# Keys and queries of two 16-head cross stages, held by head in row groups of TensorE

## The chip, the cores and the metric

The kernel runs on one core of a Trainium2 chip, as one program with one launch. The metric is the device time of one execution in microseconds; the median of three runs of the kernel before is 626.02 us (623.32 to 626.36).

## What is computed

The reference is a small transformer of twelve stages over `x` (128 rows of 128 numbers) with a context of 2048 rows of 128. Each stage adds its output to `x`. The stages are called here l0x, l0a, l0f, l1x, l1a, l1f, l2x and so on: cross attention, self attention and a feed-forward part, four times. The change is in l1x and l2x, two cross attentions of 16 heads with 8 numbers each:

```python
q = (Q @ Wq.T + bq).reshape(m, -1, H, HD)          # 128 queries, H = 16, HD = 8
k = (K @ Wk.T + bk).reshape(m, -1, H, HD)          # 2048 keys
v = (V @ Wv.T + bv).reshape(m, -1, H, HD)
energy = jnp.einsum('mqhd,mkhd->mhqk', q, k) * SCALE
energy = jnp.where(mask == 0, jnp.float32(-1e+20), energy)
attn = jax.nn.softmax(energy, axis=3)
out = jnp.einsum('mhqk,mkhd->mqhd', attn, v)
```

l2x is the same without biases and without a mask.

## The kernel before

Five engines run instruction lists written out by hand, one function per stage (`l0x`, `l0a`, ...) with a part for each engine (`@on("pe")` and so on). Engines wait for each other through semaphores that are planned by name (`Steps`). Both cross stages are one function, `cross` (L1159; its part for TensorE begins at L1192).

The products of queries and keys are made to nearly full precision from parts in the type fp32r: a number is split into a high and a low part. For a quad (four heads, `QUADS` = 4) the contraction has 105 rows (`SHOWN`): 32 rows high keys, 32 rows high keys again, 32 rows low keys (4 heads of 8 each), and 9 rows for the mask and for a shift by the maximum. Against them stands `query_r`, in which each of the 16 heads has its own 128 columns and zeros in the rows of the other three heads of its quad; `spread` (L1187) writes it, one quad on VectorE (DVE), three on GpSimd (POOL).

A stage goes twice over the scores. The first pass (`peak`) needs only the maximum of each query and head: for head h and half a, two matmuls of 512 keys each (L1218) fill two PSUM banks, and one VectorE reduce over 1024 columns (L1312) takes the maximum. There are 32 such steps in a stage. When the eight of a quad are done, `lows` is formed, `shift_gpsimd` splits it, `turn` puts it on rows by a matmul and `place` (L1325) writes it into `query_r`, so that the second pass yields scores minus the maximum.

The second pass (`score`, `weigh`) goes over 64 units, a quad and 128 keys each: one matmul, keys as weights (128 columns) and 512 columns of queries (4 heads); ScalarE (ACT) takes the exponential (L1371) from one of three PSUM banks into `probs`; `weigh` multiplies with the values in fp32, four matmuls for two units, each into its own 32 output columns of the array. `take` gathers a quad, `fold` brings the heads together.

The order on TensorE (PE) is written out: peaks 0 to 8, the first shift, two scores, peak 10, then 32 rounds v of two scores, peak v + 11 (while there are any: 21 rounds), and `weigh` of two units. Matmul records all carry line L257 (`mm`), transposes L260.

The keys come by 12 DMAs of 256 KB for each stage from `stack_keys` on SyncE's queue (SP), which copies rows from the tiles with high and low parts; l2x has one more for the constant rows.

## Time and profile before

| | |
|---|---|
| median of 3 runs | 626.02 us |
| the profiled execution | 628.98 us |
| its span, first to last instruction | 626.9 us |
| mean granted TensorE clock | 0.892 of 2.4 GHz |
| PE busy | 501.0 us (80%) |
| DVE busy | 355.9 us (57%) |
| ACT busy | 230.4 us (37%) |
| l1x / l2x, from the end of the stage before to their last sum | 80.6 to 161.9 us / 243.7 to 322.4 us |

The profile gives busy time by engine, the chain of waits that ended last, groups of instructions with their mean duration, a timeline, and busy time and granted clock for any stretch. Matmuls overlap in their pipeline, so the record of one is longer than the distance to the next; distances between starts are what counts.

### The profile page before, as it was taken

The numbers are of one execution on the slowest core, as the hardware profiler recorded it, in microseconds if no ns is written. First come the engines' busy times: TensorE is split into PE (matmuls) and PEld (weight loads), VectorE is DVE, ScalarE is ACT, GpSimd is POOL, SyncE is SP. The second block draws the span as 40 slices with busy tenths as digits, with TensorE's granted clock in tenths as the row PEclk, the third lists the DMA queues.
The fourth block names the chain that finished last, engine by engine and source line by source line (L and its number), as shares of the span: only waits on it lengthen the run. The fifth ranks groups of instructions, "written<-read, shape, count | busy, mean of one in ns | idle before, by whom it ended". The sixth has DMA issues, their size and how long they took to land.

```text
span 626.9 us, 9025 instructions
## 1 busy us (share of the span) xinstructions
PE 501.0 (80%) x3612; PEld 375.2 (60%) x3612; DVE 355.9 (57%) x795; ACT 230.4 (37%) x443; POOL 57.4 (9%) x103
## 2 busy tenths in 40 slices
PE   7778659999758707899987667778999999887786
PEld 5646534444538606444345457766888888776686
DVE  5465458771569325877446664346766666633533
ACT  7014312778014202066712124245555555511021
POOL 0210020000022011100024122200000000000000
PEclk9799956999977858599998996997999999987899
DMA  8628000000619784400020000000000000036000
GB/s 293 276 60 177 36 0 1 0 1 2 250 53 369 156 196 175 169 1 1 2 101 0 1 1 1 2 0 2 1 1 0 1 2 1 1 135 269 1 1 5
DMA packets 8004, 42.96 MB, mean 69 GB/s; under 512 B 1050, under 2 KB 4122, under 8 KB 4762
## 3 DMA queue, kind: packets, MB, share of 16 engines
q1 hardware_dynamic: 6811, 33.71, 16.4%
q0 software_dynamic: 1152, 8.68, 3.9%
q8 instruction: 28, 0.46, 0.3%
q14 instruction: 13, 0.11, 0.0%
HBM read 35.69 MB, written 0.08 MB: 57 GB/s over the span
## 4 chain that ended last, share of the span: by engine, by line
PE 57%; DVE 28%; ACT 7%; issue 4%; DMA 2%; POOL 2%; POOLq 0%; DVEq 0%; ACTq 0%
PE banks L257 52%; PE banks L260 4%; DVE small L2089 3%; ACT probs L2164 3%; DVE peaks L1312 3%; DVE weights_lo L2099 2%; DMA region<-in_tree_f,leaf_no 2%; DVE xn L343 1%; POOL mv L349 1%; DVE sbq L1546 1%; DVE probs L605 1%; ACT weights_hi L2177 1%; DVE tB L1827 1%; DVE probs L573 1%; DVE nmax L570 1%
## 5 line engine op out<-in xcount | busy, mean ns | idle before, releaser
L1312 DVE TENSOR_REDUCE peaks<-banks 128x1 f32<-128x1024 f32 x64 | 76.8, 1222 | 16.8 <-PE banks L257 16.6
L257 PE MATMUL banks<-identb 128*128 128x128 bf16 x653 | 48.0, 231 | 22.9 <-DMA region<-in_tree_f,leaf_no 15.3
L260 PE MATMUL banks<-p_first,probs 128*128 128x128 f32 x320 | 49.6, 291 | 14.5 <-DVE weights_lo L2099 5.6
L257 PEld LDWEIGHTS banks<-identb 128*128 128x128 bf16 x653 | 43.5, 105 | 27.6 <-DMA region<-in_tree_f,leaf_no 16.1
L2177 ACT CAST weights_hi<-banks 128x512 fp32r<-128x512 f32 x64 | 36.0, 587 | 56.6 <-PE banks L260 56.6
L2089 DVE TENSOR_REDUCE small<-banks 128x1 f32<-128x1024 f32 x32 | 38.9, 1217 | 28.9 <-PE banks L257 28.9
L260 PEld LDWEIGHTS banks<-p_first,probs 128*128 128x128 f32 x320 | 38.6, 149 | 25.4 <-issue 6.1
L1371 ACT ACTIVATE probs<-banks,seen 128x512 f32<-128x512 f32 x64 | 40.3, 684 | 27.6 <-PE banks L257 27.6
L2099 DVE TENSOR_TENSOR weights_lo<-banks,weights_hi 128x512 fp32r<-128x512 f32 x64 | 41.7, 682 | 13.4 <-ACT weights_hi L2177 13.4
L1371 ACT ACTIVATE probs<-banks 128x512 f32<-128x512 f32 x64 | 34.7, 595 | 32.2 <-PE banks L257 31.5
L257 PE MATMUL banks<-probs,values 128*32 128x256 f32 x512 | 41.3, 391 | 0.5 <-DVE keysT L1333 0.5
L349 POOL TENSOR_TENSOR mv<-mv,half 128x1 f32<-128x1 f32 x15 | 8.3, 551 | 336.9 <-DVE mv L341 336.9
L2164 ACT ACTIVATE probs<-banks,nmax 128x1024 f32<-128x1024 f32 x32 | 35.4, 1112 | 8.6 <-DVE nmax L2093 8.5
L257 PE MATMUL banks<-weights_hi,rows_hi 128*128 128x256 f32 x128 | 37.8, 295 | 0.0
L257 PE MATMUL banks<-weights_lo,rows_hi 128*128 128x256 f32 x128 | 36.4, 285 | 0.0
L257 PE MATMUL banks<-weights_hi,rows_lo 128*128 128x256 f32 x128 | 36.2, 283 | 0.0
L257 PE MATMUL banks<-ctx_hi,query_r 128*128 128x512 f32 x64 | 28.5, 445 | 7.9 <-ACT probs L2164 6.5
L257 PE MATMUL banks<-xnT,region 128*128 128x128 f32 (+1 forms) x226 | 32.0, 296 | 1.8 <-DVE xnT L362 1.8
L257 PEld LDWEIGHTS banks<-xnT,region 128*128 128x128 f32 (+1 forms) x226 | 29.2, 207 | 2.8 <-DVE xnT L362 2.8
L257 PE MATMUL banks<-keys_l1x,query_r 105*128 105x512 f32 x64 | 26.4, 508 | 4.3 <-DVE query_r L1189 3.2
L257 PE MATMUL banks<-keys_l2x,query_r 105*128 105x512 f32 x64 | 26.1, 504 | 3.3 <-DVE query_r L1189 2.2
L257 PE MATMUL banks<-region,probs 128*128 128x128 f32 x168 | 23.9, 287 | 3.6 <-ACT probs L682 2.1
(423 smaller groups left out, 917.0 us busy)
## 6 DMA issues: line engine op xcount, KB each, us to landing
region<-in_w_l2f SPq DMA_DIRECT2D x1, 4096.0 KB, 12.9
region<-in_w_l3f SPq DMA_DIRECT2D x1, 4096.0 KB, 11.9
region<-in_w_b SPq DMA_DIRECT2D x1, 3076.0 KB, 11.0
values<-in_ctx SPq DMA_DIRECT2D x2, 1024.0 KB, 8.5
region<-in_w_l0f SPq DMA_DIRECT2D x1, 2048.0 KB, 21.5
keys_l1x<-shared SPq DMA_DIRECT2D x8, 256.0 KB, 4.0
keys_l2x<-probsT SPq DMA_DIRECT2D x8, 256.0 KB
region<-in_w_l3d SPq DMA_DIRECT2D x1, 2048.0 KB, 17.1
```

The costliest lines, as they stand in the source:

```text
L257: return nc.tensor.matmul(o, lhsT, rhs, start=start, stop=stop)
L260: return nc.tensor.transpose(o, i, ident[0:n, 0:n])
L343: nc.vector.tensor_scalar(xn[:, :], src, mv[:, 0:1], mv[:, 3:4], ALU.subtract, ALU.mult).then_inc(V.sem, V.now(tag + ".xn"))
L349: nc.gpsimd.tensor_tensor(mv[:, 3:4], mv[:, 2:3], half[:, 0:1], ALU.pow).then_inc(G.sem, G.now(tag + ".rstd"))
L570: nc.vector.tensor_scalar(m4, m4, -scale, None, ALU.mult).then_inc(V.sem, V.now((tag, "sub", g)))
L573: nc.vector.tensor_tensor(probs[:, 1, g * BANK:(g + 1) * BANK].rearrange("p (h t) -> p h t", h=4), s, bc(nmax[:, 4 * g:4 * g + 4], 2, [P, ...
L1312: nc.vector.tensor_reduce(peaks[:, h // 4 % 2, i:i + 1], ps[:, 2 * a:2 * a + 2, :], AX.XY, ALU.max, negate=True).then_inc(VM.sem, VM.now(( ...
L1371: nc.scalar.activation(probs[:, u % 8 // 4, u % 4 * BANK:(u % 4 + 1) * BANK], ps[:, 4 + u % 3, :], ACT.Exp, scale=seen[:, 0:1] if masked e ...
L2089: return nc.vector.tensor_reduce(small[:, half:half + 1], ps[:, 2 * half:2 * half + 2, :], AX.XY, ALU.max)
L2099: nc.vector.tensor_tensor(sides(g, c, weights_lo), ps[:, 4 + c % 2, :].rearrange("p (a b) -> p a b", a=4), sides(g, c, weights_hi).bitcast ...
L2164: nc.scalar.activation(probs[:, g % 2, o:o + 2 * BANK], ps[:, 2 * half:2 * half + 2, :].rearrange("p a b -> p (a b)"), ACT.Exp, bias=nmax[ ...
L2177: nc.scalar.copy(sides(g, c, weights_hi), ps[:, 4 + c % 2, :].rearrange("p (a b) -> p a b", a=4)).then_inc(A.sem, A.now((tag, "e", g, c)))
```

## The change

Keys and queries of a quad are held by head in four groups of 32 rows. Each group has 27 rows (`ROWS_OF`): 8 high keys, 8 high keys, 8 low keys, and 3 rows for mask and shift. The queries (`packed`) are 128 rows by 512 columns for the whole stage, without zeros for other heads, so `spread` is gone.

- First pass: a step is now two heads (g = 2a, 2a + 1) over 512 keys instead of one head over 1024. Its two matmuls of 512 columns take 27 rows each, in different row groups, and write different banks. Still 32 steps, each with one reduce of 1024 columns, now to two results.
- Second pass: a unit is now one head over four tiles of 128 keys. Two units are made by eight matmuls with 27 rows, 128 weight columns and 128 moving columns each, alternating between two row groups, instead of two matmuls of 512 columns. `weigh` has the same four matmuls as before, but starts when all four units of a group are there, one round later.
- Query preparation: the weights are regrouped by ScalarE in earlier stages (`regroup`), the product of the first quad goes ahead on its own, and one ScalarE and one VectorE instruction for each of two pieces replace the copies and `spread`. The bias comes in by one more matmul for each quad in l1x.
- The shift is placed by one add of 128 x 128, from a `turn` with 128 weight columns instead of 32.
- The exponential has a constant scale in both stages; before, l1x had one from a tile.
- Loads: 48 DMAs of 64 KB for each stage instead of 12 of 256 KB; the constant rows come first. In l1x four of them stand ahead of the load of `w_l0f` on SP, behind two waits. PE waits for the keys quad by quad.

```diff
@@ stack_keys
+            if tag == "l2x":
+                for g in range(4):
+                    r = slice(32 * g + 24, 32 * g + ROWS_OF)
+                    load("rows_l2x", keys_r[tag][r, :, :]..., bc(one[r, :], 1, [ROWS_OF - 24, 4 * KT_N, P]))
             for t in range(4):
                 for part in range(3):
-                    src = (high if part < 2 else keysT[:, :])[32 * t:32 * t + 32, :]
-                    load("keys_" + tag, keys_r[tag][32 * part:32 * part + 32, t, :].bitcast(F32), src)
+                    src = high if part < 2 else keysT[:, :]
+                    for g in range(4):
+                        row = 32 * g + 8 * part
+                        load(f"keys_{tag}{t}", keys_r[tag][row:row + 8, t, :]..., src[32 * t + 8 * g:32 * t + 8 * g + 8, :]...)
@@ sp
+            sp.wait_ge(V.sem, V.at("mask.row"))
+            sp.wait_ge(A.sem, A.at(("shown", 3)))
+            for g in range(4):
+                load("rows_l1x", keys_r["l1x"][32 * g + 24:32 * g + 25, :, :].bitcast(F32), bc(keysT[96:97, :], 1, [1, 4, CTX]))
             load("w_l0f", region[:, 2 * REG:2 * REG + width(W_L0F)], dram["w_l0f"])
@@ cross, pe
                 for t in range(4):
-                    m = mm(ps[:, 4, t * P:(t + 1) * P], w("q")[:, t * P:(t + 1) * P], xnT[:, :])
-                m.then_inc(T.sem, T.now(tag + ".q"))
-                loaded(pe, "keys_" + tag)
+                    o = ps[:, 5 if t else 4, t * P:(t + 1) * P]
+                    m = mm(o, at["w_l0x"][:, t * P:(t + 1) * P], xnT[:, :], True, not masked)
+                    if masked:
+                        m = mm(o, bias_rows[:, :], ident[0:4, t:t + 1].broadcast_to([4, P]), False, True)
+                    if t in (0, 3):
+                        m.then_inc(T.sem, T.now((tag + ".q", t // 3)))
...
-                    for b in (2 * a, 2 * a + 1):
-                        m = mm(ps[:, b, :], query_r[0:SHOWN, h * P:(h + 1) * P],
-                               keys[0:SHOWN, h // 4, b * BANK:(b + 1) * BANK])
+                    for g in (2 * a, 2 * a + 1):
+                        m = mm(ps[:, g, :], packed[group(g), q * P:(q + 1) * P],
+                               keys[group(g), q, c * BANK:(c + 1) * BANK])
...
-                    mm(ps[:, 4 + u % 3, :], keys[0:SHOWN, q, t * P:(t + 1) * P],
-                       query_r[0:SHOWN, 4 * q * P:4 * (q + 1) * P]).then_inc(PU.sem, PU.now((tag, u)))
+                    for j in range(4):
+                        t = 4 * c + j
+                        for i in range(2):
+                            g = (u + i) % 4
+                            if j == 0 and u + i >= 3:
+                                pe.wait_ge(AP_.sem, AP_.at((tag, u + i - 3)))
+                            m = mm(ps[:, 4 + (u + i) % 3, j * P:(j + 1) * P], keys[group(g), q, t * P:(t + 1) * P],
+                                   packed[group(g), q * P:(q + 1) * P])
+                            if j == 3:
+                                m.then_inc(PU.sem, PU.now((tag, u + i)))
...
                     peak(v + LEAD)
-                    weigh(2 * v)
-                    weigh(2 * v + 1)
+                    if v:
+                        weigh((v - 1) // 2, (v - 1) % 2)
...
+                weigh(last // 4 - 1, 1)
@@ cross, dve
-                nc.vector.memset(hi[96:128, :], 1.0 if masked else 0.0).then_inc(V.sem, V.now(tag + ".ones"))
...
-                spread(nc.vector, 0).then_inc(V.sem, V.now((tag, "q", 0)))
+                for i in range(2):
+                    dve.wait_ge(A.sem, A.at((tag + ".qhi", i)))
+                    o = packed[:, thirds[i]]
+                    nc.vector.scalar_tensor_tensor(o, product(i), sign[:, 0:1], o.bitcast(F32), ALU.mult, ALU.add)...
...
-                    nc.vector.tensor_reduce(peaks[:, h // 4 % 2, i:i + 1], ps[:, 2 * a:2 * a + 2, :], AX.XY, ALU.max,
+                    nc.vector.tensor_reduce(peaks[:, q % 2, c, 2 * a:2 * a + 2], ps[:, 2 * a:2 * a + 2, :], AX.X, ALU.max,
...
+                    nc.vector.tensor_tensor(o, turned(q), o.bitcast(F32), ALU.add).then_inc(VQ.sem, VQ.now((tag, q)))
```

## Rows read from the trace of the kernel before

**Rows 1.** The page's chain that ended last, shares by engine.

```profile
PE 57%; DVE 28%; ACT 7%; issue 4%; DMA 2%; POOL 2%; POOLq 0%; DVEq 0%; ACTq 0%
```

**Rows 2.** The chain in order of time, l1x: start us, us, what.

```profile
116.23 12.96 PE banks L257 x88
...
147.61 10.21 PE banks L257 x88
```

**Rows 3.** Windows: length; busy PE, PEld, DVE, ACT, POOL; granted clock; DMA share; GB/s.

```profile
89.50:102.50 13.00, 11.31 (x22) 4.89 (x21) 11.51 (x11) 0.00 (x0) 2.69 (x5) 0.50 0.00 0
102.50:106.30 3.80, 3.80 (x13) 2.56 (x16) 2.45 (x2) 2.52 (x4) 0.00 (x0) 0.50 0.00 0
106.30:109.70 3.40, 3.40 (x28) 1.66 (x32) 2.45 (x2) 1.92 (x5) 0.00 (x0) 0.99 0.02 5
...
116.00:130.50 14.50, 14.23 (x99) 6.70 (x98) 11.16 (x13) 10.27 (x17) 0.39 (x2) 1.00 0.00 1
```

**Rows 4.** Timeline, one round of the second pass: start, us, engine, line, operation.

```profile
120.29 3.48 DVE L1312 TENSOR_REDUCE peaks<-banks 128x1 f32<-128x1024 f32 x3
120.60 0.16 PEld L257 LDWEIGHTS banks<-probs,values 128*32 128x32 f32 x8 [0.36 <-DVE keysT L1333]
120.60 0.64 PE L257 MATMUL banks<-probs,values 128*32 128x256 f32 x8
...
121.17 0.73 PE L257 MATMUL banks<-query_r,keys_l1x 105*128 105x512 f32 x2
...
121.72 1.26 ACT L1371 ACTIVATE probs<-banks,seen 128x512 f32<-128x512 f32 x2 [0.43 <-PE banks L257]
121.75 0.63 PE L257 MATMUL banks<-keys_l1x,query_r 105*128 105x512 f32 x2
...
122.30 0.64 PE L257 MATMUL banks<-probs,values 128*32 128x256 f32 x8
```

**Rows 5.** Timeline, rounds without first-pass work, in l1x and l2x.

```profile
148.72 7.43 ACT L1371 ACTIVATE probs<-banks,seen 128x512 f32<-128x512 f32 x12 [0.26 <-PE banks L257]
...
150.65 0.74 PE L257 MATMUL banks<-query_r,keys_l1x 105*128 105x512 f32 x2
...
151.89 0.73 PE L257 MATMUL banks<-query_r,keys_l1x 105*128 105x512 f32 x2
...
309.62 2.31 ACT L1371 ACTIVATE probs<-banks 128x512 f32<-128x512 f32 x4 [0.45 <-PE banks L257]
```

**Rows 6.** Timeline, query preparation in l1x and l2x.

```profile
83.78 2.08 PE L257 MATMUL banks<-xnT,p_w_a 128*128 128x128 f32 x8 [0.38 <-DVE xnT L362]
85.90 1.12 ACT L1362 ACTIVATE keysT<-banks,p_cols 96x128 fp32r<-96x128 f32 x4 [11.16 <-PE banks L257]
...
88.22 0.69 DVE L1189 TENSOR_TENSOR query_r<-keysT,p_const 128x512 fp32r<-128x512 f32 x1
...
246.87 1.16 PE L257 MATMUL banks<-xnT,region 128*128 128x128 f32 x8 [0.38 <-DVE xnT L362]
...
249.39 0.69 DVE L1189 TENSOR_TENSOR query_r<-keysT,p_const 128x512 fp32r<-128x512 f32 x1
```

**Rows 7.** Timeline, consecutive fp32r matmuls of 256 columns in l3x.

```profile
435.56 0.28 PE L257 MATMUL banks<-weights_hi,rows_lo 128*128 128x256 f32 x1
435.68 0.28 PE L257 MATMUL banks<-weights_hi,rows_hi 128*128 128x256 f32 x1
```

**Rows 8.** Timeline of SyncE's queue: issues of small and of large DMAs.

```profile
37.90 0.33 SPq L302 DMA_DIRECT2D distance_rows<-dists  x1
...
216.47 2.59 SPq L283 DMA_DIRECT2D keys_l2x<-probsT  x2
```

**Rows 9.** The page's time to landing, and a window during the last gather.

```profile
region<-in_tree_q,leaf_no POOLq DMA_INDIRECT x2, 6.9
...
222.90:230.00 7.10, 0.00 (x0) 0.00 (x0) 0.00 (x0) 0.00 (x0) 1.87 (x2) 0.50 0.82 110
```

**Rows 10.** Timeline of VectorE in l0x, the mask row.

```profile
15.25 1.28 DVE L722 TENSOR_SCALAR keys_l1x<-shared,seen 1x2048 fp32r<-1x2048 f32 x1
```

More of the change, by code:

```diff
@@ L223, in build @@
                   *("leaf1_" + t for t in "qkvf"),
-                  *("leaf2_" + t for t in "qkvf"), "w_b", "w_c", "w_l2f", "l2f_b2", "w_l3f", "w_l3d", "ctx2", "bias", "keys_l1x", "keys_l2x")}
+                  *("leaf2_" + t for t in "qkvf"), "w_b", "w_c", "w_l2f", "l2f_b2", "w_l3f", "w_l3d", "ctx2", "bias", "rows_l1x", "rows_l2x",
+                  *(f"keys_{c}{t}" for c in ("l1x", "l2x") for t in range(4)))}
         load_n = {}
@@ L852, in _ @@
                 for t in range(4):
-                    nc.scalar.copy(keys_r["l1x"][96:128, t, :].rearrange("p (a b) -> p a b", b=P),
-                                   bc(one[96:128, :], 1, [32, KT_N, P])).then_inc(A.sem, A.now(("shown", t)))
+                    nc.scalar.copy(keys_r["l1x"][:, t, :].rearrange("p (a b) -> p a b", b=P),
+                                   bc(one[:, :], 1, [P, KT_N, P])).then_inc(A.sem, A.now(("shown", t)))
                 ctx_scalar(act, tag, 1, 1.0)
@@ L886, in _, with regroup @@
                                  1.0).then_inc(G.sem, G.now("pairs"))
+        def regroup(src, name):
+            for t in range(4):
+                c = slice(t * P, (t + 1) * P)
+                m = nc.scalar.copy(at["w_l0x"][:, c].rearrange("p (g r d) -> p g r d", g=4, r=4),
+                                   src[:, c].rearrange("p (r g d) -> p g r d", r=4, g=4))
+            m.then_inc(A.sem, A.now(name))
         def l0a():
@@ L901, in l0a @@
             V.plan(("l1x", "low", 2), "l0a.c", ("l1x", "low", 3))
-            A.plan(*(("l1x", "k", b) for b in range(NB)))
+            A.plan(*(("l1x", "k", b) for b in range(NB)), "l1x.wq")
             T.plan("l0a.y")
@@ L977, in _ @@
                     keys_scalar(act, "l1x", at["l1x_bk"], b, 2 + b % 2, shared)
+                act.wait_ge(T.sem, T.at("l0x.y"))
+                regroup(at["w_l1x_q"], "l1x.wq")
             @on("pool")
@@ new lines, in weigh @@
+                def weigh(w, half):
+                    q, c = w // 4, w % 4
+                    if c == 0 and q and not half:
+                        pe.wait_ge(VO.sem, VO.at((tag, q - 1)))
+                    pe.wait_ge(AP_.sem, AP_.at((tag, 4 * w + 3)))
+                    of = probs[:, w % 2, :].rearrange("p (g j n) -> p g j n", g=4, j=4)
+                    for j in (2 * half, 2 * half + 1):
+                        t = 4 * c + j
+                        for i in range(2):
+                            r = 32 * (2 * (t % 2) + i)
+                            v = t * VW + (2 * q + i) * PW
+                            m = mm(ps[r:r + 32, 7, 0:2 * P].rearrange("p (h n) -> p h n", h=2), values_t[:, v:v + 32],
+                                   of[:, 2 * i:2 * i + 2, j, :], t < 2, t >= KT_N - 2)
+                    m.then_inc(PV.sem, PV.now((tag, w, half)))
@@ L1263, in _ @@
                 peak(9)
-                score(0)
-                score(1)
+                scores(0)
                 peak(10)
@@ L1376, in _ @@
                 norm_gpsimd(pool, tag)
-                if not masked:
-                    nc.gpsimd.memset(shifts[:, :, 0:1].rearrange("p s c -> p (s c)"), 0.0)
-                pool.wait_ge(V.sem, V.at(tag + ".qs"))
-                for t in range(1, 4):
-                    spread(nc.gpsimd, t).then_inc(G.sem, G.now((tag, "q", t)))
+                gl(pool, nc.gpsimd.memset(shifts[:, :, :], 0.0))
                 for q in range(QUADS):
@@ L1677, in _ @@
                                      accum_out=s[:, 2:3]).then_inc(A.sem, A.now("l1f.p"))
+                loaded(act, "w_b")
+                act.wait_ge(T.sem, T.at(("l1x.q", 1)))
+                regroup(at["w_b.l2x_q"], "l2x.wq")
                 tree_scalar(act, "f", ACT.Gelu)
```

206 lines of the change are left out of this document (95 added, 111 removed).

## The prediction

> **What bounds the kernel now.** I read the page's chain first: TensorE (PE) holds 57% of the span, VectorE (DVE) 28% [rows 1]. The chain in order of time then shows where. In l1x and in l2x it runs in long unbroken pieces of PE: 12.96 us for a quad of the second pass with first-pass work beside it, 10.21 us for the last quad [rows 2]. Third, the windows. From 89.5 to 102.5 us only first-pass steps run: DVE is busy 11.51 of 13.0 us and PE 11.31, at a granted clock of 0.50, so each waits for the other in turn. In 116.0 to 130.5 us PE is busy 14.23 of 14.5 us at full clock, DVE 11.16, ACT 10.27 [rows 3]. That stretch is bound by PE. Last, the timeline of one round: `weigh` starts at 120.60 us, two scores at 121.17, the peak pair at 121.75, the next `weigh` at 122.30: 0.57 + 0.58 + 0.55 = 1.70 us [rows 4]. The last 10 or 11 rounds have no peak and take 151.89 - 150.65 = 1.24 us, of which ACT's two exponentials are busy 1.24 in l1x (7.43 / 6) and 1.16 in l2x (2.31 / 2) [rows 5]. What the change is worth is read from these rounds: 21 with a peak and 11 without in each stage.
>
> **What a matmul costs.** In l3x fp32r matmuls of 256 columns, each with its own 128-column weights, follow each other every 0.12 us at full clock [rows 7]. So 512 columns stream in 0.23 us, 128 in 0.06, and a load of 128 weight columns takes no more than 0.12 when it is beside other work. Two matmuls of 512 would be 0.46; in the round they take 0.57 and 0.55 [rows 4], so some 0.11 us is left each time for the first load and for going from 128 to 32 output columns and back.
>
> **First pass, steady part.** The two matmuls of a peak step lie in different row groups. Side by side they take 0.23 + 0.11 = 0.34 us instead of 0.55 to 0.58; one after the other there is no gain. The trace has no two matmuls in different row groups. The nearest row is `weigh`: its eight weight loads in four column groups are all done within 0.16 us, and its eight matmuls of 256 columns within 0.64 [rows 4], where eight alone at the 0.12 of [rows 7] would be 0.96 even if fp32 were as quick. I take side by side.
>
> **Second pass.** Two units cost eight loads and eight matmuls of 128 columns instead of two of 512. The columns that stream are the same in sum, but the loads are four times as many. If a pair loads and streams at once, it goes at 0.06 (stream bound) to 0.12 (load bound): 0.11 + 4 x 0.11 = 0.55 us for two units, 0.35 at best. If the loads of a pair go one after the other at 0.115, it is 0.11 + 8 x 0.115 = 1.03. I take 0.55, by the column groups of `weigh`. `weigh` stays 0.57. A round with a peak is then 0.55 + 0.34 + 0.57 = 1.46 us of PE, bounds 1.26 and 1.94 (1.03 + 0.34 + 0.57).
>
> Other bounds of a round: DVE's reduces stand three in 3.48 us, 1.16 each [rows 4]; with some 1.2 us a quad for `lows`, `place` and `take` a round is 1.16 + 0.15 = 1.31, so DVE bounds if PE falls below that. ACT needs 1.16. The ring of three banks makes a loop: the first exponential starts 121.72 - 121.17 = 0.55 us after its score's start; now the last piece starts 0.33 later and streams 0.17 less, so 0.71, plus 0.58 for the exponential (2.31 / 4) and 0.05 to the next score: 1.34. With peaks it is hidden behind PE. Without them it ends last: 1.34 instead of 1.24.
>
> Gain: 21 x (1.70 - 1.46) = 5.0 us; loss: 11 x 0.10 = 1.1 us, and 0.57 for a whole `weigh` group that is now left behind the last exponential. Net 3.4 us a stage at full clock.
>
> The Trainium skill ("TensorE: Matmul & The Clock Gate", section on LDWEIGHTS) says that a load's time goes by its columns, columns / 1.2 ns, and that 32 rows load no quicker than 128: an estimate of 107 ns for each of the 256 loads, against 64 before. Its page "TensorEngine Tiling (Array Packing)" (Key Properties) says that different tiles load and multiply in parallel. By the first alone two units would take about 0.97 us, which is the third case below; by both, 0.54.
>
> **Query preparation.** Before, eight matmuls (2.08 us in l1x), four copies on ACT, four on DVE and the 0.69 us spread stand between 83.78 and 88.22 + 0.69 = 88.91 us, 5.1 us; in l2x from 246.87 to 250.08, 3.2 us [rows 6]. After, the first peak waits for the products of all quads on PE's own queue (16 matmuls in l1x with the bias, about 3.8 us by 2.08 / 8 each less their overlap; 1.16 us in l2x), and DVE must write the second piece before its first reduce (about 1.1 us for one ACT and one DVE instruction of 384 columns, by the 0.69 for 512). So the first reduce can begin some 5 us after the start of the products in l1x (before, 6.5: 5.1 and one slow pair of matmuls) and 2.3 in l2x (before, 4.6). Saving: l1x 1.5, l2x 2.3 us. A `memset` of 0.48 us ahead of the norm also goes (0.4). On POOL the three spreads go; nobody waits for them.
>
> **First steps.** DVE's wait of 13.0 - 11.51 = 1.5 us in the window [rows 3] shrinks, since a pair is back sooner: 0.9 us, bounds 0 and 1.5.
>
> **The clock.** In 102.5 to 106.3 us the second pass starts at 0.50 (1.2 GHz) and the clock is granted in full from 106.3 on; in the 13 us before, 87% busy with a pause at every reduce, it was not [rows 3]. After the change each score pair streams 128 columns for a load of 128, so PE multiplies less of the time, above all at 1.2 GHz, where the scores of a round might take 1.0 us for 0.43 us of columns. I expect the full clock some microseconds later: 2 us a stage, bounds 0 and the second case below.
>
> **Loads.** 48 issues at the 0.33 us of a small one [rows 8] to 0.45 are 16 to 22 us, against 15 us before in issues of 1.3 us (2.59 / 2) [rows 8]. They start when the low keys are there and l1x has some 40 us of cover. In l2x they run from 206.8 to some 230 us, beside the gather of the last tree. That one already waits: from 222.9 to 230 only 110 GB/s flow at a DMA share of 0.82, beside the 512-byte pieces of the constant rows [rows 9], and it lands after 11.4 us, where the gather of the first tree took 6.9 [rows 9]. The constant rows now go first, so the gather meets larger pieces: I take -1 us, bounds -4.5 (6.9 instead of 11.4) and +4 (shared until 234). Only if the keys of a quad came late would PE wait; the first reduce needs them at 248. On SP the load for l0f stands behind the mask row, written at 16.5 us [rows 10]; 45 us of l0a and l0f cover it. In l0a a small matmul and a copy are added on the path: +0.3. `regroup`, eight copies on ACT, lies in stretches where ACT waits: nothing, 1.2 us a stage if it did not.
>
> **Sum.** l1x: -3.4 - 1.9 - 0.9 + 2.0 = -4.2. l2x: -3.4 - 2.7 - 0.9 + 2.0 = -5.0. With -1.0 and +0.3: -9.9 us. The profiled execution took 628.98 us (span 626.9), so 619.1; against the median of 626.02 it is 616.1 us.
>
> **The rivals.** First, all goes better: pairs at 0.06, DVE bounds the round at 1.31, the full clock comes as soon as before, the gather is freed. 21 x 0.39 = 8.2 for 5.0, the loop 0.16 shorter (11 x 0.16 = 1.8), the clock 2.0: 7.0 us a stage more, 602 us.
>
> Second, and slower: the clock. If PE's pauses keep the grant at 0.50, a round at 1.2 GHz is about 1.0 + 0.5 + 1.1 = 2.6 us instead of 1.70, one without peak 2.1 instead of 1.24: 21 x 0.9 + 11 x 0.86 = 28 us, less 3 of preparation, 25 us for a stage. It decides from the point at which a round's multiplying share is as low as that of the first pass, which stayed at 0.50 for 13 us [rows 3]. For it: 2 x 0.43 us of streaming in each 1.27 us of first-pass work is two thirds, and a slow round would be (0.43 + 0.43 + 0.85) / 2.6, also two thirds. Against it: pauses in the slow round may be shorter (scores at 0.6 us give 0.78), and `weigh` has none. The skill's page on the clock gate (Part 1) says that recent activity alone sets the grant, which agrees with rows 3; with it the second pass would lift the clock late or not at all. Against the forecast's -4.2 that is 29 us: one stage held 645 us, half of its second pass 631, both stages 675.
>
> Third, the pairs do not load side by side: a round of 1.94 and a loop of 0.55 + 0.77 - 0.17 + 0.63 = 1.8: 21 x 0.24 + 11 x 0.56 = 11.2 us a stage lost, with the last `weigh` 11.8; the rest wins 0.8 and 1.6 in the two stages and 0.7 beside them: 626.0 + 23.6 - 3.1 = 646.5 us.
>
> Fourth, the change does not do what it says: pairs are not side by side anywhere, but loads are hidden, a round stays near 1.7 and only the preparation is won: 621 to 626.
>
> **How the numbers follow.** Forecast case 0.42 (610 to 620), first rival 0.16, second 0.22 (0.12 of it for one stage or part of one, 0.10 for both), third 0.10, fourth 0.10. The likeliest time is 616.1. The range leaves out the both-stages case and a little below the best: 602 to 648. About 0.5% (3.1 us) is what a measurement of this kernel can tell from no change. Faster: 0.42 + 0.16 + 0.04 of the fourth = 0.62; within 0.5%: the other 0.06; slower: 0.22 + 0.10 = 0.32.
>
> **What would show it.** In the changed trace: distance between `weigh` groups in a quad with peaks (1.46); starts of two matmuls of a peak step within some 0.02 us of each other; distance of score pairs (0.11); granted clock in the 10 us after the first score; the rounds without peak (1.34); the first reduce 1.9 us (l1x) and 2.7 us (l2x) nearer to the end of the norm; landing of the last gather. Wrong would be above all a clock of 0.50 in the second pass, or score pairs at 0.23.

## The result, and the profile after

The changed kernel takes 685.45 us, the median of four runs (683.49 to 687.38), where the kernel before, on the same chip, took 625.88 (623.32 to 626.36). The ratio is 1.0956, with a 95% interval of 1.0913 to 1.1. I had predicted 616.1 us, in a range of 602 to 648, so forecast and range are both wrong; what came is the second rival, the clock at its low level in both stages, for which I had worked out 675 us and given 0.10. The profiled execution has a span of 681.7 us (before, 626.9) and a mean granted clock of 0.781 (before, 0.892). The ratios here and below leave out executions over 1.5% above the fastest of the same kernel: one of four in e3 (928.39 us), two of four in e10, two of ten in e11, and two of seven of the kernel before beside e1, e3 and e4.

The page of the profile first: TensorE's clock in 40 slices of the span, tenths of full speed. The first line is of the kernel before, the second of the changed one.

```profile
PEclk9799956999977858599998996997999999987899
```

```profile
PEclk9779855555597966755555988698999999977889
```

Before, the clock is low for a slice or two at the start of each cross stage (slices 6 and 7, and 17). After, it is low in two long blocks, slices 6 to 11 and 18 to 22: they are l1x as a whole and l2x but for its first microseconds. The chain that ended last (the first line gives its shares; then start, length, what) says that TensorE holds both second passes without a break; [rows 2] has the pieces of before:

```profile
PE 61%; DVE 24%; ACT 6%; issue 3%; DMA 3%; POOL 1%; SPq 0%; POOLq 0%; DVEq 0%; ACTq 0%
```

```profile
84.37 5.84 PE banks L260 x18
91.56 9.06 DVE peaks L1346 x8
101.49 2.34 PE banks L260 x9
104.47 81.25 PE banks L260 x479
...
252.10 16.77 DMA region<-in_tree_f,leaf_no
269.72 5.70 PE banks L260 x34
280.87 9.06 DVE peaks L1346 x8
290.79 2.34 PE banks L260 x11
293.77 80.57 PE banks L260 x480
```

The windows of the changed kernel (columns as in [rows 3]):

```profile
91.50:101.00 9.50, 5.55 (x14) 2.03 (x14) 9.47 (x11) 0.71 (x1) 0.05 (x1) 0.50 0.11 43
104.50:130.50 26.00, 26.00 (x175) 13.97 (x177) 14.33 (x15) 11.27 (x21) 0.40 (x2) 0.50 0.00 1
130.50:170.00 39.50, 39.50 (x278) 21.18 (x282) 15.81 (x20) 16.59 (x31) 0.79 (x4) 0.50 0.00 1
170.00:185.70 15.70, 15.68 (x116) 8.86 (x108) 0.00 (x0) 6.23 (x12) 0.00 (x0) 0.50 0.01 2
274.50:281.30 6.80, 3.87 (x39) 3.05 (x38) 3.16 (x10) 2.20 (x3) 0.85 (x2) 1.00 0.51 99
281.30:373.50 92.20, 88.10 (x584) 47.63 (x588) 41.72 (x46) 34.99 (x65) 1.58 (x8) 0.50 0.19 63
```

The second passes are 100% busy at 0.50, which is 1.2 GHz. The kernel before got its full clock back at 106.3 us, 3.8 us after its first scores [rows 3]; here it does not come back in 80 us of unbroken work. And in l2x the clock was granted in full as the stage began (274.5 to 281.3) and was lost within it. (Before, too, the first pass of l2x lost it, at 249.7 us, but there the second pass had it back at 266.8.) "Busy" hides the difference: the page of the profile counts a TensorE as busy that spends half of a score pair waiting for weights. One round shows that (start, us, engine, line, operation; answers to [rows 4]):

```profile
120.76 0.79 PE L260 MATMUL banks<-keys_l1x,query_r 27*128 27x512 f32 x2
...
121.48 1.08 PE L260 MATMUL banks<-probs,values 128*32 128x256 f32 x8
121.60 1.22 DVE L1346 TENSOR_REDUCE peaks<-banks 128x2 f32<-128x1024 f32 x1 [0.44 <-PE banks L260]
122.49 0.71 PEld L260 LDWEIGHTS banks<-query_r,keys_l1x 27*128 27x128 f32 x6 [0.81 <-issue]
122.49 0.69 PE L260 MATMUL banks<-query_r,keys_l1x 27*128 27x128 f32 x4
...
124.07 1.08 PE L260 MATMUL banks<-probs,values 128*32 128x256 f32 x8
```

The two matmuls of a pair start 3 ns apart, so pairs do run side by side. But a pair of 128 columns takes 0.213 us at 1.2 GHz, and the columns are half of that (512 take 0.427 there, in the blocks of e2). The rest is the load: in e2 a 128-row matmul of 256 columns also takes 0.213 at that clock, so its load hides behind 256 columns and not behind 128. From one `weigh` group to the next (121.48 to 124.07) it is 2.587 us, and 2.054 us in the rounds without a peak; before, 1.70 and 1.24.

Where the 54.8 us between the two spans lie: 1.0 before l1x (the filler matmuls of the identity beside its norm start at 81.60 us, before at 80.62); 26.9 in l1x (its last piece ends at 185.72, before at 157.82); 3.5 from there to the norm of l2x (the last gather alone is 16.77 - 11.43 = 5.3 longer, the rest 1.8 shorter); 24.2 in l2x (from norm to last piece 98.6, before 74.4); and -0.8 behind it. The rounds alone give 21 x (2.587 - 1.70) + 11 x (2.054 - 1.24) = 27.6 us a stage.

### The profile page after: what moved, and what is told of

It is laid out like the page before. It is cut to its first block, busy times and chain, and to the rows that moved or that the text cites. A ratio compares the mean times of both kernels' runs of the same rounds, so it can differ in the third digit from the quotient of the medians.

```text
span 681.7 us, 9892 instructions
## 1 busy us (share of the span) xinstructions
PE 555.7 (82%) x4006; PEld 413.3 (61%) x4006; DVE 350.5 (51%) x790; ACT 227.3 (33%) x450; POOL 51.7 (8%) x100
## 4 chain that ended last, share of the span: by engine, by line
PE 61%; DVE 24%; ACT 6%; issue 3%; DMA 3%; POOL 1%; SPq 0%; POOLq 0%; DVEq 0%; ACTq 0%
PE banks L260 57%; PE banks L263 4%; DVE small L2114 3%; ACT probs L2189 3%; DVE peaks L1346 3%; DMA region<-in_tree_f,leaf_no 2%; DVE weights_lo L2124 2%; DVE xn L355 1%; POOL mv L361 1%; DVE sbq L1567 1%; DVE probs L617 1%; ACT weights_hi L2202 1%; DMA ctxT<-in_ctxT 1%; DVE tB L1852 1%; DVE xnT L374 1%
## 5 line engine op out<-in xcount | busy, mean ns | idle before, releaser
L1396 ACT ACTIVATE probs<-banks 128x512 f32<-128x512 f32 x128 | 69.5, 595 | 108.2 <-PE banks L260 108.2
L1346 DVE TENSOR_REDUCE peaks<-banks 128x2 f32<-128x1024 f32 x64 | 77.0, 1222 | 47.6 <-PE banks L260 47.4
L260 PE MATMUL banks<-probs,values 128*32 128x256 f32 x512 | 68.0, 628 | 0.0
L260 PEld LDWEIGHTS banks<-identb 128*128 128x128 bf16 x653 | 44.9, 107 | 28.6 <-DMA region<-in_tree_f,leaf_no 16.6
L260 PEld LDWEIGHTS banks<-query_r,keys_l1x 27*128 27x128 f32 x256 | 29.6, 317 | 24.8 <-ACT probs L1396 22.2
L260 PEld LDWEIGHTS banks<-query_r,keys_l2x 27*128 27x128 f32 x256 | 29.6, 317 | 24.8 <-ACT probs L1396 22.2
L260 PE MATMUL banks<-query_r,keys_l1x 27*128 27x128 f32 x256 | 35.6, 426 | 0.2 <-ACT probs L1396 0.2
L260 PE MATMUL banks<-query_r,keys_l2x 27*128 27x128 f32 x256 | 35.6, 426 | 0.2 <-ACT probs L1396 0.2
```

The source lines that it names most:

```text
L260: return nc.tensor.matmul(o, lhsT, rhs, start=start, stop=stop)
L1346: nc.vector.tensor_reduce(peaks[:, q % 2, c, 2 * a:2 * a + 2], ps[:, 2 * a:2 * a + 2, :], AX.X, ALU.max, negate=True).then_inc(VM.sem, VM. ...
L1396: nc.scalar.activation(probs[:, u % 8 // 4, u % 4 * BANK:(u % 4 + 1) * BANK], ps[:, 4 + u % 3, :], ACT.Exp, scale=scale).then_inc(AP_.sem, ...
```

## The experiments

Two theories. A: the clock goes by the share of the time in which columns stream; the short matmuls with a load each, and the pauses, lower it. B: how many of the 128 rows of the array are in use counts as well; the change streams through 54 rows where before there were 105. Beside them, the loads of the keys and the gather.

The runs were made on four chips, and the kernel before, run beside them, had medians of 627.1 us (e1 to e4), 626.24 (e5, e6), 631.47 (e7 to e10) and 626.84 (e11, e12). So differences between runs of different groups are good to some microseconds only; the ratios are to the kernel before on the same chip. e2, e5 and e12 were executed once each, and where a trace is read it is one execution. The code cuts show the main lines of an edit; `...` marks what is left out.

**e1_burst.** 48 small matmuls of 128 rows ahead of the first scores of each stage.

```diff
                 peak(9)
+                keep(48, 7)
                 scores(0)
```

> The changed kernel with 48 bf16 matmuls of 128 columns (full array, some 5 us at 1.2 GHz) put on TensorE right before the first scores of each of the two stages; nothing else differs. Theory A (the full clock is not granted because a round at 1.2 GHz, 2.59 us, multiplies only two thirds of its time, but once granted it is kept): granted clock 1.0 for the rest of the second pass, a round with a peak near 1.46 us and one without near 1.34, about 27 us less in each stage: 631 us. Theory B (paired matmuls of 27 rows do not count as work enough to keep the clock, whatever the time they take): the clock falls back to 0.50 within some microseconds and the time is 680 to 690 us. Theory C (the clock is only half of the loss: loads of a pair go one after the other): full clock but rounds of 1.9 us, about 650 us.

689.83 us (685.44 to 690.98), ratio 1.1009 [1.0921, 1.1097]. The burst did lift the clock, in both stages, and it did not last:

```profile
103.50:107.90 4.40, 4.40 (x43) 4.40 (x44) 1.23 (x1) 0.00 (x0) 0.00 (x0) 0.50 0.01 4
107.90:111.30 3.40, 2.70 (x37) 2.01 (x35) 1.89 (x2) 2.15 (x4) 0.00 (x0) 1.00 0.00 0
111.30:130.00 18.70, 18.70 (x129) 9.62 (x127) 9.60 (x10) 7.63 (x15) 0.40 (x2) 0.50 0.00 1
...
299.00:302.40 3.40, 2.70 (x34) 1.99 (x31) 2.13 (x2) 2.22 (x5) 0.00 (x0) 1.00 0.92 362
302.40:380.00 77.60, 77.60 (x543) 41.76 (x544) 28.16 (x33) 32.53 (x60) 1.18 (x6) 0.50 0.05 12
```

So it is no matter of getting started: the rounds of the change don't hold the full clock either. The 3.4 us at full clock show what a round's parts cost there:

```profile
108.31 0.66 PE L260 MATMUL banks<-query_r,keys_l1x 27*128 27x128 f32 x9
108.75 0.19 PEld L260 LDWEIGHTS banks<-keys_l1x,query_r 27*128 27x128 f32 x2
```

Four score pairs take 108.75 - 108.31 = 0.44 us, 0.11 each, as I had put them.

**e2_blocks.** Seven blocks of matmuls behind the last stage, each after a pause of 10 us.

```diff
+                if i == 1:
+                    for k in range(32):
+                        m = mm(ps[:, k % 4, :], src[rows(0), 0:P], src[rows(0), BANK:2 * BANK])
...
+                if i == 4:
+                    for k in range(64):
+                        m = mm(ps[:, k % 4, 0:P], src[:, 0:P], src[:, BANK:BANK + P])
...
```

> The changed kernel with seven blocks of TensorE work added behind the last stage, each after a pause of some 10 us in which TensorE rests (clock 0.50): 0: 32 fp32r matmuls of 128 rows and 512 columns; 1: the same with 27 rows; 2: 32 pairs of 27 rows in two row groups, 512 columns; 3: 64 such pairs with 128 columns each; 4: 64 matmuls of 128 rows with 128 columns; 5: 64 of 128 rows with 256 columns; 6: 48 pairs of 27 rows with 256 columns. Theory A (what counts is the share of time in which columns stream): blocks 0, 1, 2, 5 and 6 lift the clock to 1.0 within some microseconds, blocks 3 and 4 do not, because each matmul of 128 columns waits 0.21 us for its weights at 1.2 GHz and streams for 0.11. Theory B (what counts is the part of the array in use): blocks 0 and 5, perhaps 4, lift it; 1, 2, 3 and 6 do not. Starts of a pair within 0.01 us of each other in block 2.

In order: 128 rows and 512 columns (its stretch before and after the lift); 27 rows and 512; two groups of 27 rows side by side, 512; the same with 128 columns; 128 rows and 128 columns; 128 rows and 256 columns, after the lift; two groups of 27 rows, 256:

```profile
687.80:693.80 6.00, 5.97 (x14) 4.77 (x15) 0.00 (x0) 0.00 (x0) 0.00 (x0) 0.50 0.00 0
693.80:698.00 4.20, 4.20 (x19) 3.24 (x18) 0.00 (x0) 0.00 (x0) 0.00 (x0) 1.00 0.00 0
708.70:722.10 13.40, 13.40 (x32) 10.20 (x32) 0.00 (x0) 0.00 (x0) 0.00 (x0) 0.50 0.00 0
733.20:746.60 13.40, 13.40 (x64) 10.38 (x64) 0.00 (x0) 0.00 (x0) 0.00 (x0) 0.50 0.01 1
757.70:771.20 13.50, 13.50 (x128) 13.50 (x128) 0.00 (x0) 0.00 (x0) 0.00 (x0) 0.50 0.01 1
782.10:795.60 13.50, 13.50 (x64) 13.50 (x64) 0.00 (x0) 0.00 (x0) 0.00 (x0) 0.50 0.00 0
809.80:815.90 6.10, 6.05 (x51) 5.85 (x49) 0.00 (x0) 0.00 (x0) 0.00 (x0) 1.00 0.01 3
826.30:837.00 10.70, 10.61 (x96) 10.31 (x96) 0.00 (x0) 0.00 (x0) 0.00 (x0) 0.50 0.00 0
```

Both theories have a part. The 27-row block streams without a pause, 32 matmuls of 512 columns in 13.4 us (0.42 each, the speed of 1.2 GHz), and is not lifted, nor is the block with 54 rows: B. The block of 128 rows and 128 columns is bound by its loads, half of its time streams, and it is not lifted either, while the same rows with 256 columns for a load are lifted after 3.4 us: A. The time was 839.03 us, with the blocks.

**e3_hybrid.** First pass in pairs as in the change, second pass on all rows with 512 columns as before it. (The constant rows of l2x are written as in e4.)

```diff
...
+                    mm(ps[:, 4 + u % 3, :], keys[:, q, t * P:(t + 1) * P], wide(q)).then_inc(PU.sem, PU.now((tag, u)))
...
```

> Only the first pass keeps the two heads side by side; the second pass multiplies as the kernel before did, one matmul of 512 columns for four heads and 128 keys over all 128 rows, from queries spread by head (one VectorE instruction of 128 x 512 for each quad, after the shift). The constant rows of the second stage's keys are written by GpSimd instead of 512-byte DMAs. Theory A: at 1.2 GHz a round multiplies 2.1 of 2.6 us, the clock is lifted within some microseconds as before the change, a round takes about 1.48 us (0.57 scores, 0.34 peak, 0.57 weigh) instead of 1.70: 605 to 617 us. Theory B (paired 27-row matmuls hold the clock down wherever they are): clock 0.50 in the second pass, over 660 us.

692.15 us, ratio 1.107 [1.0969, 1.117]: no quicker than the change itself. The window of the second pass:

```profile
103.00:174.80 71.80, 67.86 (x282) 24.78 (x282) 32.06 (x36) 26.06 (x48) 1.18 (x6) 0.50 0.00 1
```

A round takes 2.887 us from one `weigh` to the next, longer than in the change. Its parts are full-width scores of 0.43 each, a pair of 512 columns, `weigh`, and about half a microsecond in between, where TensorE goes over from 27-row pairs to `weigh` and to the full width; "0.65 <-issue" stands before such a load in the timeline. With the first pass in pairs the clock stays low for 72 us of l1x, though the second pass has its old matmuls. Whether that is the rows or these pauses, the run doesn't tell.

**e4_ones.** The constant rows of l2x written by GpSimd instead of loaded in pieces of 512 bytes.

```diff
...
-                    load("rows_l2x", keys_r[tag][r, :, :].rearrange("p t (a b) -> p (t a) b", b=P).bitcast(F32),
-                         bc(one[r, :], 1, [ROWS_OF - 24, 4 * KT_N, P]))
...
+                    nc.gpsimd.memset(keys_r["l2x"][:, t, :].bitcast(F32), 1.0).then_inc(G.sem, G.now(("l2x", "ones", t)))
```

> The changed kernel; only the constant rows of the second stage's keys are written by GpSimd instead of four DMAs in pieces of 512 bytes. Theory A: the last gather, which takes 16.8 us after the change and 11.4 before it, is slowed by the pieces of SyncE's queue that are still in flight; with them gone it lands 4 to 9 us earlier and the time is 676 to 682 us, with the clock in the second pass still at 0.50. Rival: the gather is slowed by the 48 key copies themselves; then less than 2 us are won.

687.28 us, ratio 1.0976 [1.0895, 1.1058], no gain. That is the rival guess; the first one is out, as the gather is longer still. The 48 loads of the keys, which stood behind the pieces, are issued 7.7 us earlier (from 237.22 us, in the change from 244.93), so more of them are under way beside it; e8 tests whether the loads are the reason:

```profile
252.72 21.76 DMA region<-in_tree_f,leaf_no
```

**e5_rows.** Thirteen more blocks: which numbers of rows are lifted, and which hold.

```diff
+                if i == 1:
+                    for k in range(32):
+                        m = one(slice(0, 96), BANK, k % 4)
...
+                if i == 8:
+                    warmed(24)
+                    for k in range(64):
+                        m = one(rows(0), BANK, 4 + k % 4)
...
```

> The changed kernel with thirteen blocks of fp32r matmuls behind its last stage, each after a pause of 10 us in which TensorE does nothing. Blocks 1 to 8 and 13 start at the low clock: 128 rows of ones and zeros in bf16, 512 columns; 96 rows; 64 rows; four groups of 27 rows side by side; 27 + 27 + 64 rows side by side; two tiles of 64 rows side by side; 128 rows with 32 output columns; 128 rows with 64 output columns; and last two tiles of 64 rows with 256 columns. Blocks 9 to 12 start with 24 matmuls of 128 rows and 512 columns, which lift the clock, and go on with 64 of 27 rows, 64 pairs of 27 rows, 64 of 64 rows, or 192 of 128 rows and 128 columns each. Theory A (the share of the time in which columns stream sets the clock): blocks 1 to 8 and 13 all stream without a pause, so all are lifted to 2.4 GHz after some microseconds, and 9 to 11 stay there for their 14 us; only block 12, half loading, may fall. Theory B (how many of the 128 rows are in use counts as well): block 1 and the two tiles of 64 rows are lifted, 27 and 54 rows are not held (blocks 9 and 10 fall back to 1.2 GHz within some 5 us), and the blocks of 64, 96 and 108 rows show where between the two it turns. With 32 and 64 output columns theory B says nothing; if these are not lifted, it is the used part of the whole array that counts and not its rows.

From the low clock: 96 rows (720.4 on), 64 rows (741.1), four groups of 27 side by side (765.6), 27 + 27 + 64 rows (786.0), two tiles of 64 (842.8). Then, after a lift by 24 matmuls of 128 rows: 27 rows (from 913.2; the full clock ends at 917.3), pairs of 27 (from 955.2), and 128 rows with 128 columns (from 1022.2); the last two windows begin with what is left of the 24.

```profile
726.20:730.50 4.30, 4.30 (x20) 3.33 (x18) 0.00 (x0) 0.00 (x0) 0.00 (x0) 1.00 0.00 0
741.10:754.80 13.70, 13.66 (x32) 10.31 (x32) 0.00 (x0) 0.00 (x0) 0.00 (x0) 0.50 0.00 1
...
770.50:775.20 4.70, 4.70 (x88) 4.33 (x80) 0.00 (x0) 0.00 (x0) 0.00 (x0) 1.00 0.01 3
786.00:832.00 46.00, 46.00 (x96) 18.27 (x96) 0.00 (x0) 0.00 (x0) 0.00 (x0) 0.50 0.00 0
...
849.00:853.00 4.00, 4.00 (x38) 3.47 (x34) 0.00 (x0) 0.00 (x0) 0.00 (x0) 1.00 0.00 0
...
917.30:937.00 19.70, 19.70 (x48) 15.04 (x46) 0.00 (x0) 0.00 (x0) 0.00 (x0) 0.50 0.00 0
...
951.40:969.90 18.50, 18.50 (x145) 15.11 (x144) 0.00 (x0) 0.00 (x0) 0.00 (x0) 1.00 0.00 1
...
1019.70:1043.50 23.80, 23.80 (x204) 23.32 (x202) 0.00 (x0) 0.00 (x0) 0.00 (x0) 1.00 0.01 1
```

The whole took 1065.56 us. 64 rows were not lifted; 96, 108 and twice 64 were (the last with 256 columns too, after 3.1 us). At full clock 27 rows fell back after 4.1 us and 54 held to the end of their block, 14.8 us, as 64 did; 128 rows with 128 columns held for 21.5 us, where from the low clock they had not been lifted. Theory B had the 54 rows fall, and theory A had allowed it for the 128 columns; both held. Columns of the array did not matter: 128 rows with 32 or 64 output columns were lifted like the rest. So it is rows that count, and not the used part of the whole array; nor do row groups side by side keep the clock down as such, since four of 27 and two of 64 were lifted. One surprise: the trios of 27 + 27 + 64 rows took 46 us instead of 14, 0.72 us for each change between a 32-row and a 64-row matmul, with no overlap between them. They use 118 rows, but each 0.72 us has only 0.43 of columns, and they were not lifted in all of the 46 us.

**e6_tiles.** The way out that this suggests: two tiles of 64 rows, each with two heads. A copy of the queries in which the other head's rows are zero lets a peak pair use all 128 rows, and a score matmul take two heads as 256 columns for one load. (The constant rows of l2x are written as in e4, VectorE and GpSimd write the copy, and a `weigh` group starts when two units are there and no longer waits for four.)

```diff
-                        m = mm(ps[:, g, :], packed[group(g), q * P:(q + 1) * P],
-                               keys[group(g), q, c * BANK:(c + 1) * BANK])
+                        m = mm(ps[:, 2 * a + i, :], wide[q][tile_of(i), a, :],
+                               keys[tile_of(i), q, c * BANK:(c + 1) * BANK])
...
+                            m = mm(ps[:, 4 + (u + i) % 3, 2 * j * P:2 * (j + 1) * P].rearrange("p (h n) -> p h n", h=2),
+                                   keys[tile_of(i), q, t * P:(t + 1) * P], wide[q][tile_of(i), :, :])
```

> Both passes of the changed kernel in two tiles of 64 rows instead of four groups of 27. A tile holds two heads; their queries stand beside each other in a copy in which the other head's rows are zero, so every pair of matmuls uses all 128 rows, and a score matmul streams 256 columns for one load instead of 128. Added: one split on VectorE and three on GpSimd a stage, one small VectorE addition a quad; the constant rows of l2x come from GpSimd. Theory B (rows in use): the clock comes back in the second pass as it did before the change (within some 5 us of its start). A round is then scores 0.11 + 2 x 0.12 = 0.35, peak 0.34, weigh 0.57 = 1.26 us of TensorE, so that VectorE's 1.3 us bounds it; 21 x 0.4 = 8 us a stage less than before the change, about 605 to 612 us in all. Theory A (share of streaming time): in a slow round scores 0.43 + 0.1, peak 0.43 + 0.1, weigh 1.07, streaming 0.9 of the time, so the clock comes back too; this run alone doesn't tell the theories apart, the one with the blocks does. If neither holds the clock stays at 0.5 for 90 us a stage and the time is about 2.15 us a round: 665 us.

618.34 us (614.07 to 622.12), ratio 0.9873 [0.9798, 0.9948]. The clock comes back at 108.5 us and at 265.5, 6.9 and 7.5 us after the first scores of the two stages (3.7 and 3.0 in the kernel before):

```profile
102.00:108.50 6.50, 6.41 (x40) 3.10 (x38) 5.26 (x5) 4.34 (x8) 0.00 (x0) 0.50 0.01 3
108.50:130.00 21.50, 19.61 (x210) 9.22 (x206) 19.36 (x24) 15.57 (x29) 0.80 (x4) 1.00 0.00 1
```

A round takes 1.24 us (`weigh` at 119.93 and 121.17 in its timeline), bound by VectorE: its reduces have 71.9% of the chain that ended last between 108.5 and 130 us, though TensorE is busy 19.61 us there too. The time is 6 us above my range; the gather took 20.0 us, and e7 takes that up.

**e7_tiles_gather.** The same, and the keys of quads 1 to 3 of l2x loaded only when the last gather has landed.

```diff
             for t in range(4):
+                if tag == "l2x" and t == 1:
+                    loaded(sp, "leaf1_f")
+                    loaded(sp, "leaf2_f")
```

> The kernel in two tiles of 64 rows again, with one edit: of the 48 small loads that stack the keys of l2x, those of quads 1 to 3 wait until the last gather (tree_f) has landed. In the run without this edit that gather took 20.0 us beside the loads, before the change 11.4, and the first gather of the kernel before, alone, took 6.9. If the loads hold the gather back, it lands within 7 to 9 us of its issue and the time falls by 10 to 12 us, to 606 to 609. Rival: the gather is slow by itself at this place, then it still takes 15 us or more and the time stays at 618. Second rival: the keys of quad 1 come too late (36 loads of 0.66 us begin at about 223 us, 12 of them are done at 231, all at 247), then TensorE waits at the first peak of a quad.

606.5 us (603.59 to 609.3), ratio 0.9653 [0.9566, 0.9739] to the kernel before: the best of all, 11.8 us better than e6 by the medians, on another chip (by the ratios, 14). The first row is e6, the second e7:

```profile
215.81 20.04 DMA region<-in_tree_f,leaf_no
```

```profile
215.82 6.19 DMA region<-in_tree_f,leaf_no
```

No peak of a quad waits for its keys: the first eight reduces of l2x follow each other from 236.34 for 9.14 us. In l2x the first pass loses the clock (240.6 us) and the second has it back at 254.2:

```profile
240.60:254.20 13.60, 11.01 (x48) 5.48 (x52) 11.91 (x14) 3.94 (x8) 0.39 (x2) 0.50 0.77 123
```

The same kernel was run once more, on another chip (e12_tiles_warm).

> The kernel in two tiles of 64 rows with the late loads once more, as it was, for a second profile beside a second chip: 603 to 609 us, the clock back within 12 us of the first score in l1x and before the first score in l2x.

It took 605.75 us. In l1x the clock was back 8.7 us after the first score, as expected; in l2x it was back at 257.3 us, 7.8 after the first score (249.5) and not before it.

**e8_change_gather.** The changed kernel with the edits of e4 and e7.

> The changed kernel with the constant rows of l2x from GpSimd and the keys of quads 1 to 3 of l2x loaded after the last gather. The clock is not touched: it stays at 0.5 in both second passes. The gather lands within 7 to 9 us instead of 16.8 (21.8 with the constant rows from GpSimd alone): 675 to 678 us. That prices the loads in my sum, where I had put -1 us.

674.57 us, ratio 1.0743 [1.0657, 1.083]; the gather lands after 5.87 us. Against the change that is 10.9 us less by the medians (on another chip; by the ratios, 13), about as much as the gather is shorter (16.77 - 5.87 = 10.9). So it is the loads that hold the gather back, e4's rival guess. The clock stays at 0.5 for 102 us of l1x and 96 of l2x.

**e9_tiles_27rows.** e6 with the 27 rows of one head in a peak pair.

```diff
-                        m = mm(ps[:, 2 * a + i, :], wide[q][tile_of(i), a, :],
-                               keys[tile_of(i), q, c * BANK:(c + 1) * BANK])
+                        r = slice(64 * i + 32 * a, 64 * i + 32 * a + ROWS_OF)
+                        m = mm(ps[:, 2 * a + i, :], wide[q][r, a, :],
+                               keys[r, q, c * BANK:(c + 1) * BANK])
```

> The kernel in two tiles of 64 rows, with one edit: the matmuls of the first pass use only the 27 rows of their own head again. Instructions, columns, loads and waits are the same in number and length; only the rows in use in a peak pair fall from 128 to 54. Theory A (share of time in which columns stream): nothing changes, 618 us. Theory B (rows in use count as well): the clock comes back later or, more likely, not before the peaks end, because the slow round then has a third of its streaming time with 54 rows, as the run with the first pass paired and the second full had: each stage loses 20 to 30 us against 618, so 655 to 675 us.

663.66 us, ratio 1.0552 [1.0469, 1.0635], 45 us more than e6 by the medians, on another chip (by the ratios, 43). In l1x the clock stays low until the last peaks of the stage are done and some 6 us longer, in l2x some 2:

```profile
120.00:165.10 45.10, 45.10 (x262) 18.71 (x256) 22.63 (x28) 19.53 (x36) 0.79 (x4) 0.50 0.00 1
165.10:176.00 10.90, 10.16 (x112) 5.49 (x110) 1.10 (x4) 7.58 (x14) 0.00 (x0) 1.00 0.01 2
```

I had written that only the rows change. That is not so: a round takes 2.46 us, about 0.3 more than the first one of e6 at the low clock (107.645 - 105.484 = 2.16), because TensorE now goes from 64-row to 32-row matmuls and back ("0.22 <-issue" before the peak's load). So the run shows that the first pass's pairs of 27 rows alone keep the clock down; how much of it is rows and how much these pauses, it leaves open. The blocks, which have no pauses, show that rows alone can do it.

**e10_tiles_128col.** e6 with each score matmul cut in two of 128 columns with a load each, all rows in use.

> The kernel in two tiles of 64 rows, with one edit: each score matmul of 256 columns becomes two of 128 with a load each, as in the change. All 128 rows stay in use. At the low clock a pair takes 0.21 us of which half streams, so scores take 0.85 us instead of 0.43 a round, as in the change. If the loads matter by themselves (half-streaming scores), the clock stays at 0.5 through the second pass: 660 us or more. If only the rows in use matter, the clock comes back some microseconds later than in the kernel with 256 columns and then holds; rounds are 0.11 + 8 x 0.06 to 0.115 / 2, at most 0.25 us longer: 622 to 630 us.

666.03 us (654.86 to 685.43), ratio 1.0462 [1.0344, 1.058]. In the profiled run, which took 671.61 us, the clock stays at 0.5 for 105.8 us of l1x as in the change, with the change's own round of 2.587 us; in l2x it came back after 54.6:

```profile
130.00:170.00 40.00, 40.00 (x284) 21.09 (x282) 16.36 (x21) 17.36 (x32) 0.80 (x4) 0.50 0.01 1
```

The executions differ by 30 us, and the longer one took, the lower was its mean granted clock: 0.834, 0.825, 0.810 and 0.784. Even the two quickest (654.86 and 660.44) are 36 us and more above e6, whose clock was 0.871 to 0.880. So the loads alone, with all rows in use, keep it down as well, though less surely; where in the stages the quickest lost it, no trace shows.

**e11_before_gather.** The kernel before with the edit of e7.

> The kernel before the change with the one edit of the gather: the loads that stack the keys of quads 1 to 3 of l2x, and the constant rows behind them, wait until tree_f has landed. The gather took 11.4 us there and 5.9 to 6.2 us in the two kernels with this edit. The keys of l2x have one semaphore in this kernel, and the first peak waits for all of them: 10 loads, begun some 6 us earlier than the gather landed before. Expected: the gather lands 4 to 5 us sooner; the keys are then stacked by about 229 + 13 + the constant rows, some 8 us, so 245 to 250 where the first peak wants them at 246: 621 to 626 us. It shows how much of the 606.5 us is this edit alone: if it is 5 us, the tiles are worth some 20.

636.92 us, ratio 1.0126 [1.008, 1.0172]: some 1% slower, where I had expected 621 to 626. The gather lands after 7.6 us instead of 11.4, but this kernel waits for all keys at once, and the constant rows end last:

```profile
219.52 7.60 DMA region<-in_tree_f,leaf_no
...
236.94 10.94 DMA keys_l2x<-one
```

The edit pays only with keys that are counted quad by quad, which the change brought.

## Why the prediction was wrong

Step by step.

- **Pairs side by side:** right. Starts 3 ns apart; 0.11 us a score pair at full clock (e1).
- **The round at full clock, 1.46 us:** never seen, as the full clock lasted 3.4 us in the second pass of e1 and not at all in that of the change. Of its parts the scores were right (0.50 us from the first to the peak pair, for 0.55); the tiles, with other matmuls, reached 1.24.
- **The clock, 2 us a stage:** this is the step that failed, with 27.6 us of rounds a stage in its place. I took the kernel before's return at 106.3 us as the rule and asked only how much later it would come. My own second rival had the numbers: a slow round of 2.6 us (measured 2.587), without a peak 2.1 (2.054), a multiplying share of two thirds, as low as in the stretch that had stayed at 0.50. I set against it that scores might take 0.6 us; they take 0.85, four pairs of 0.213, bound by their loads. And I did not see what e2 and e5 show, that rows out of use count too, so the change stood worse than that share. e9 (with its pauses) and e10 show that each of the two, put into e6 by itself, keeps the clock down. So 0.10 for both stages was far too little, the more so as the mechanism is the same in both; their shares in the change's own loss stay open.
- **The rule on recent activity**, which I cited from the Trainium skill ("TensorE: Matmul & The Clock Gate", Part 1), is not refuted, but the page tells of activity as being busy. Here a block busy 13.40 of 13.40 us in 27 rows was not lifted; the measurement decides.
- **675 against 685:** about half of the 10 us is which executions are compared: the medians differ by 59.6 us, the profiled executions by 683.49 - 628.98 = 54.5, and the rival has 49. Of the other 5.5, 4.5 lie between the two stages (3.5, where I had -1.0 for the gather) and 1.9 in the stages beside the rounds (-0.7 and -3.4, where I had -3 each); the rest is under 1 us a piece. The next steps have the parts.
- **Query preparation:** in l1x a loss of 0.7 us instead of a gain of 1.5: the products, each followed by its 4-row bias matmul, take 5.84 us on the chain where I had 3.8. The two matmuls of a product and the two of its bias start 0.72 us apart, as the trios of e5 do, where two loads would need 2 x 0.213 = 0.43; seven such changes between 128 and 4 rows are an estimated 2.0 us, which is the difference. The first reduce comes 91.56 - 84.37 = 7.2 us after their start, before 6.5. In l2x the first reduce comes 5.0 us after the start of the norm's statistics, before 7.1: 2.1 gained, where I had 2.3 (the `memset` stood ahead of them).
- **First steps:** right. The first eight reduces stand back to back, 9.06 us or 1.13 each, and DVE's wait is gone.
- **Loads:** I had -1 us with a bound of +4; the gather took 5.3 us more. The constant rows did not clear the way, and the key loads stretch over it. I had put a load's issue at 0.33 to 0.45 us; it takes 0.66 (5.29 / 8), and in l2x the 52 issues take 49.5 us (234.7 to 284.2), where I had some 23. Without the pieces and with three quarters of the loads held back the gather takes 5.9 to 6.2 us (e7, e8): 10.9 us were to be had in the change. In the kernel before the same gather went from 11.4 to 7.6, and the time did not follow (e11).
- **l0a:** +0.3 expected; l1x starts 1.0 later.
- **What bounds the kernel:** right, and it is why e6 and e7 pay. TensorE's rounds went from 1.70 to 1.24 us there, the value at which I had said VectorE would bound.

## What to carry to other kernels

Before packing small contractions into row groups, work out the slow round: at 1.2 GHz, how long do loads and pauses last beside the columns, and through how many of the 128 rows do they stream? If that is no more than in a stretch of the same trace that stayed at 0.50, expect the clock to stay down, and price that level for all such stages together. Fill the rows instead, with zeros if need be: two heads in a 64-row tile with 256 columns for one load gave what four groups of 27 rows had promised. And let small loads that are needed late wait for a gather that is needed now: 20.0 us became 6.2. That paid only where the loads were counted quad by quad.

## What the runs showed of the hardware that I had not expected

- A TensorE that is busy all the time is not always lifted to 2.4 GHz: 27, 54 and 64 rows with 512 columns were not in 13.4 to 13.7 us, 96, 108 and 128 were after 4.9 to 6.2. Once there, 54 and 64 rows held it for the 14.8 us of their blocks, 27 fell after 4.1.
- 128 rows with 128 columns for each load were not lifted in 13.5 us, and held the full clock for 21.5 us when they had it.
- Output columns had no such part: 128 rows by 32 columns were lifted after 5.7 us.
- Zeros did not count as idleness: a bf16 block of the identity alone was lifted after 5.8 us.
- Row tiles of different sizes did not run side by side: 0.72 us for each 512-column matmul at 1.2 GHz instead of 0.43. The Trainium skill ("TensorEngine Tiling (Array Packing)", Key Properties) says that a change of tiling mode drains the engine; the trios of e5 agree.
- The indirect gather shares badly with many small transfers: 5.9 to 7.6 us with few loads issued ahead of it and none beside it, 11.4 behind 13 loads, one of them in 512-byte pieces, 16.8 to 21.8 with the 48 loads under way.
